# Delta-rule attention and expert layer: key groups 1 and 2 projected in the merging, query group 5 in the recurrence

## The reference, cut to what matters

```python
def _short_conv(x, w):
    K = w.shape[-1]
    L = x.shape[1]
    xp = jnp.pad(x, ((0, 0), (K - 1, 0), (0, 0)))
    y = sum((xp[:, t:t + L, :] * w[:, t] for t in range(K)))
    return jax.nn.silu(y)
...
q = _short_conv(hidden_states @ Wq.T, qconv_w).reshape(B, L, H, -1)
k = _short_conv(hidden_states @ Wk.T, kconv_w).reshape(B, L, H, -1)
v = _short_conv(hidden_states @ Wv.T, vconv_w).reshape(B, L, H, -1)
beta = jax.nn.sigmoid(hidden_states @ Wb.T)
delta, _S = _delta_rule(tr(q), tr(k), tr(v), jnp.swapaxes(beta, 1, 2))
...
short = _fir_conv(v, fir_short_w)
longp = _fir_conv(v, fir_long_w)
paths = (short, longp, delta, v)
gate_in = jnp.concatenate([hidden_states] + [stats(p) for p in paths], -1)
hmid = jax.nn.gelu(gate_in @ gate_w1.T + gate_b1, approximate=False)
logits = hmid @ gate_w2.T + base_bias.reshape(-1)
...
out = sum((probs[..., i, None] * p for i, p in enumerate(paths)))
out = out * jax.lax.rsqrt(jnp.mean(out * out, -1, keepdims=True) + 1e-05) * onorm_w
return out.reshape(B, L, -1) @ Wo.T
```

## Time and profile before

| what | value |
|---|---|
| median of 3 runs | 1901.33 us (1894.56 to 1901.97) |
| the profiled execution's own time | 1894.72 us |
| its span, first to last instruction | 1893.0 us |
| mean granted TensorE clock | 0.904 of full |
| busy: PE, DVE, ACT, POOL | 79%, 69%, 50%, 23% of the span |
| stage B, by the first and last softmax | 428.20 us to 1343.83 us |

### The profile page before, as it was taken

How to read it: one execution, slowest core, us unless ns; L and a number is a source line. 1 busy time by engine, 2 the same in 40 slices (tenths; PEclk the granted TensorE clock), 3 DMA queues, 4 the chain that set the end, 5 groups by cost and what they waited for, 6 DMA issues and landing times. The chain is left out here.

```text
span 1893.0 us, 40332 instructions
## 1 busy us (share of the span) xinstructions
PE 1496.2 (79%) x12507; PEld 1108.8 (59%) x12508; DVE 1315.3 (69%) x3331; ACT 950.1 (50%) x1998; POOL 440.7 (23%) x473
## 2 busy tenths in 40 slices
PE   6775165979999999999999999887436999999800
PEld 3445134747747747657557567476225888888700
DVE  6995155677787887887887887875455555554488
ACT  6772061356555644654655555542443555555434
POOL 6884200000030040040030210300223333333300
PEclk9997585989999999999999999998758999999955
DMA  5558642023243243333333333232524533333295
GB/s 197 190 163 256 154 101 58 3 67 94 71 127 92 62 122 102 78 91 101 87 89 106 95 106 90 79 97 76 196 91 140 192 105 101 104 104 101 77 385 190
DMA packets 297370, 224.34 MB, mean 119 GB/s; under 512 B 173472, under 2 KB 265632, under 8 KB 296960
## 3 DMA queue, kind: packets, MB, share of 16 engines
q1 hardware_dynamic: 225600, 158.84, 29.0%
q0 software_dynamic: 15232, 43.53, 6.4%
q10 hardware_dynamic: 56384, 19.93, 4.1%
HBM read 130.42 MB, written 91.82 MB: 117 GB/s over the span
## 5 line engine op out<-in xcount | busy, mean ns | idle before, releaser
L1462 DVE SCALAR_TENSOR_TENSOR B_conv<-B_ps_x,B_cw,B_conv 128x511 f32<-128x511 f32 (+2 forms) x192 | 143.5, 748 | 65.9 <-ACT B_conv L1176 59.3
L2031 POOL DMA_INDIRECT y_d<-C_yb,C_dest x136 | 132.1, 971 | 232.0 <-ACT C_yb L2142 229.7
L422 POOL DMA_INDIRECT xs_d<-x,slot_u x128 | 133.4, 1042 | 137.4 <-DVE m_acc L1857 100.6
L688 POOL MEMSET B_z<- 128x256 f32 (+4 forms) x40 | 5.5, 191 | 674.6 <-DMA B_z<-scr_a 674.6
L1176 ACT ACTIVATE B_conv<-B_ps_x,B_cw 128x512 f32<-128x512 f32 x64 | 43.7, 683 | 167.6 <-PE B_ps_x L745 167.3
L2261 DVE TENSOR_TENSOR C_av<-C_sg,C_ps_g 128x256 f32<-128x256 f32 x136 | 57.3, 421 | 94.6 <-ACT C_sg L2136 94.6
L2065 PE MATMUL C_ps_g<-C_w_high,C_xt_high 128*128 x272 | 119.5, 439 | 0.4 <-issue 0.4
L745 PE MATMUL B_ps_x<-B_xa,B_wk 128*128 128x512 f32 x128 | 67.5, 655 | 63.8 <-DVE B_sel L1454 44.9
L2273 DVE TENSOR_TENSOR C_avt_low<-C_ps_a,C_avt_high 128x256 fp32r<-128x256 f32 x136 | 57.7, 425 | 83.5 <-ACT C_avt_high L2131 83.5
L2065 PE MATMUL C_ps_g<-C_w_high,C_xt_low 128*128 x272 | 107.7, 396 | 0.0
L2065 PE MATMUL C_ps_g<-C_w_low,C_xt_high 128*128 x272 | 107.0, 393 | 0.0
(11 more groups left out here) (330 smaller groups left out, 4250.6 us busy)
## 6 DMA issues: line engine op xcount, KB each, us to landing
C_xb<-xs_d SPq DMA_DIRECT2D x136, 132.0 KB, 2.1
C_w_high<-y_d SPq DMA_DIRECT2D x12, 1024.0 KB, 14.1
A_band<-fir_long POOLq DMA_DIRECT2D x32, 256.0 KB, 5.9
A_work<-xT SPq DMA_DIRECT2D x16, 512.0 KB, 5.0
v_d<-A_v_tok SPq DMA_DIRECT2D x16, 512.0 KB, 3.5
short_d<-A_sh_tok SPq DMA_DIRECT2D x16, 512.0 KB, 3.2
B_xa<-xT SPq DMA_DIRECT2D x8, 1024.0 KB, 5.8
B_v_tok<-v_d SPq DMA_DIRECT2D x8, 1024.0 KB, 5.5
```

Of the source, the lines that this page charges most:

```text
L422: pool.indirect_dma_start(t["xs_d"][:, :], bass.IndirectOffsetOnAxis(ap=slot_u[:, c:c + 1], axis=0), x1[:, b, j, :], None).then_inc(done, 16)
L1462: V.scalar_tensor_tensor(conv[:, g % 2, k:], X[g % 2][:, :SEQ - k], cw[:, g // 4, gg % CH, 3 - k:4 - k], conv[:, g % 2, k:], ALU.mult, ALU ...
L2031: pool.indirect_dma_start(t["y_d"][:, :], bass.IndirectOffsetOnAxis(ap=dest[:, q:q + 1], axis=0), yb[:, u], None).then_inc(y_out[u], 16)
```

## The change

Every group is taken one place earlier. Groups 1 and 2 of the next pair are projected in `merges`, where two `spin` fillers stood (one of the two came later in it and is moved up), and `group_a(i+2, 1)` on ACT comes with them. In the recurrence, groups 3, 4 and 5 are projected in place of 2, 3 and 4; on DVE the taps of group 1 stand first, and those of groups 4 and 5 later. `stage1b` loses group 5 on all three engines. The `bn` rows of the values are spread over the first block. Three other things are changed:

- The gate's first four products (columns 0 and 1 of half 0, `hidden_from_x`) are made in `stage1b` in place of a `spin(B3, 2)` and a `spin(B3, 3)`.
- POOL's mask waits for the first weighed paths of the mixing (`mixd`) and no longer for the solved blocks read back (`mt_in`).
- PE's first projection of a step no longer waits for the solver's store (`x_out`), and the `spin(X[1], 4)` that ended a step stands behind it.

```diff
                 def mask_at(p):
                     pool.wait_ge(at_kept, 8 * (p + 1))
-                    pool.wait_ge(mt_in[1], 32 * (p + 1))
+                    need(pool, mixd, 4 * (p - 1) + 1)
...
+                def hidden_from_x(i, c):
+                    pe.wait_ge(xg_in[0], 16 * (i + 1))
+                    for k in range(CH):
+                        mm(X[c % 2][:], w1x[:, k, c * P:(c + 1) * P], xg[0][:, k, :], start=k == 0, stop=False)
...
                     turn_norms(p, 0)
-                    project(p, 5)
...
-                            spin(B3, 2)
+                            if g != 6:
+                                spin(B3, 2)
+                        if g == 6 and not first:
+                            pe.wait_ge(taps, 24 * p + 21)
+                            hidden_from_x(p - 1, 0)
...
                         rank(last)
-                        spin(B3, 3)
+                    if not first:
+                        pe.wait_ge(taps, 24 * (p + 1))
+                        hidden_from_x(p - 1, 1)
...
-                    if has_prev:
-                        spin(X[1], 2)
+                    if has_next:
+                        project(i + 1, 1)
...
-                    if has_prev:
-                        spin(X[1], 3)
+                    if has_next:
+                        project(i + 1, 2)
...
-                    if has_next:
-                        project(i + 1, 1)
...
                         if has_next:
-                            project(i + 1, s + 1)
+                            project(i + 1, s + 2)
...
-                        for k in range(CH):
-                            mm(X[c % 2][:], w1x[:, k, c * P:(c + 1) * P], xg[b][:, k, :], start=k == 0, stop=False)
+                        if b or c > 1 or not has_next:
+                            for k in range(CH):
+                                mm(X[c % 2][:], w1x[:, k, c * P:(c + 1) * P], xg[b][:, k, :], start=k == 0, stop=False)
...
                     if has_next:
-                        hold(pe, x_out, 16 * (i + 1))
                         project(i + 1, 0)
+                    if has_prev:
+                        spin(X[1], 4)
                     merges(i, has_prev, has_next)
...
                         at_rest(i + 1)
-                        spin(X[1], 4)
...
                         for k in (1, 2):
                             merge(i + 1, k)
+                    if has_after:
+                        group_a(i + 2, 1)
                     rms(i, 0)
...
-                    for q in range(TPB):
-                        bn(q, 2)
+                    if has_next:
+                        taps_of(i + 1, 1)
+                    bn(0, 2)
                     state(0)
-                    if has_next:
-                        taps_of(i + 1, 1)
+                    bn(1, 2)
                     output(0)
...
                     output(2)
+                    if has_next:
+                        taps_of(i + 1, 4)
...
-                        taps_of(i + 1, 4)
+                        taps_of(i + 1, 5)
```

More of the change, by code:

```diff
@@ L809, in at_products, with stage1b @@
                                 i.then_inc(at_mm, 1)
-                def stage1b(p, last=None):
+                def hidden_from_x(i, c):
+                    pe.wait_ge(xg_in[0], 16 * (i + 1))
+                    for k in range(CH):
+                        mm(X[c % 2][:], w1x[:, k, c * P:(c + 1) * P], xg[0][:, k, :], start=k == 0, stop=False)
+                def stage1b(p, last=None, first=False):
                     if last is not None:
@@ L1008, in gate @@
                     for c in range(HID_CH):
-                        if b == 0 and c == 0:
-                            pe.wait_ge(taps, 24 * (i + 2) if has_next else 24 * (i + 1))
+                        if b == 0 and c == 0 and not has_next:
+                            pe.wait_ge(taps, 24 * (i + 1))
                         if not (b == 0 and c < 2):
                             pe.wait_ge(gelu_ok, 4 * half + c - 1)
-                        for k in range(CH):
-                            mm(X[c % 2][:], w1x[:, k, c * P:(c + 1) * P], xg[b][:, k, :], start=k == 0, stop=False)
+                        if b or c > 1 or not has_next:
+                            for k in range(CH):
+                                mm(X[c % 2][:], w1x[:, k, c * P:(c + 1) * P], xg[b][:, k, :], start=k == 0, stop=False)
                         if c == 0:
@@ L1107, in _ @@
                 turn_betas(0)
-                for g in range(1, 5):
+                for g in range(1, 6):
                     project(0, g)
@@ L1111, in _ @@
                         select(0, g - 2)
-                select(0, 3)
-                stage1b(0)
+                stage1b(0, first=True)
                 at_first(0)
@@ L1213, in stage1b @@
                 def stage1b(p, last=None):
-                    group_a(p, 5)
                     for j in range(4):
@@ L1296, in recur @@
                         group_b(i + 1, 0)
-                        group_a(i + 1, 1)
+                        group_a(i + 1, 2)
                     for s in range(1, TPB):
@@ L1300, in recur @@
                             group_b(i + 1, s)
-                            group_a(i + 1, s + 1)
+                            group_a(i + 1, s + 2)
                         if has_prev and s == 3:
@@ L1396, in _ @@
                     group_b(0, g)
+                group_a(0, 5)
                 root_squares(0, 0)
@@ L1401, in _ @@
                 load_solved(0)
-                for k in range(5):
+                for k in range(3):
+                    merge(0, k)
+                group_a(1, 1)
+                for k in range(3, 5):
                     merge(0, k)
@@ L1492, in stage1b @@
                     keep_k(p, 3)
-                    taps_of(p, 5)
                     dve.wait_ge(beta_ok, 2 * (p + 1))
@@ L1604, in output @@
                                         ALU.mult).then_inc(r_out, 1)
-                    for q in range(TPB):
-                        bn(q, 2)
-                    state(0)
                     if has_next:
                         taps_of(i + 1, 1)
+                    bn(0, 2)
+                    state(0)
+                    bn(1, 2)
                     output(0)
@@ L1618, in recur @@
                         bn(0, 3)
+                    bn(2, 2)
+                    bn(3, 2)
                     residual(1)
@@ L1857, in place @@
                     V.tensor_tensor(m_acc[:], m_acc[:], m_sum[:], ALU.add).then_inc(rt, 1)
-                for g in range(5):
+                for g in range(6):
                     taps_of(0, g)
```

## The result

The changed kernel takes 1908.19 us, median of 9 runs (1905.17 to 1912.86); the kernel before, beside it, 1901.33 (9 runs, 1890.82 to 1903.05). The ratio is 1.0059, with a 95% interval of 1.0039 to 1.0078: slower, where a gain of 1.3% had been forecast. The profiled execution took 1908.19 us, its span is 1906.4 us, the mean granted clock 0.887 (0.904 before).

What follows compares the result with a forecast made beforehand. DVE's own program was taken to bound stage B. Gains of 2.7 + 0.9 + 0.2 = 3.8 us a step, 19 us over five middle steps, plus 5 elsewhere, took 24 us off 1901.33: 1877 us, range 1864 to 1896.

Steps and rivals of the forecast that it cites:

- First taps: Start of a step: projection ahead of the filler lets ACT start sooner; DVE's 1.46 us wait shrinks, gain 0.85 us.
- Merging: Second merge: of 3.4 us gained earlier, 1.5 in hand plus 1.2 from PE starting sooner get through, 2.7 us.
- gains stopped by PE: Rival, chance 0.22: solved blocks no sooner, PE's jump shows, clock takes the recurrence's part; 11.5 us gained, 1890 us.
- Mask: `add_two` (L1725) no longer stands still for POOL's mask, taps not slowed: gain 1.2 us in a middle step.
- Softmax: Gate work about 1.8 us sooner: logits' wait goes, exponentials' wait falls to 0.38 us; gain 1.3 us a step.
- Recurrence and stage 1b: Taps of group 1 wait no more, group 5's move in: 0.9 us gained in the recurrence, 0.2 in `stage1b`.
- The 3 us before `keep_even`: Sign in `stage1b`: without group 5's taps, `keep_even` waits about 3.2 us in place of 1.10.
- The clock: PE ahead of the first solved rows: nearly 4 us wait, clock falls in most steps; by the skill about 1880 us.
- The slow rival: Rival, chance 0.10: clock low from L919 until after the second residual, 36 us lost against 24 gained, 1913 us.
- The sum: Whole kernel: 3.8 us a step, 19 us for five middle steps, 5 us at the ends; 24 us in all.

Runs made afterwards that it cites:

- e1: The changed kernel with the filler put back from behind the first projection to the end of the step: 1881.37 us, ratio 0.9912 to the kernel before.
- e2: The kernel before with only the filler moved behind the first projection, which no longer waits for the memory's outputs: 1914.48 us, ratio 1.0082.
- e11: The changed kernel with the filler in both places, at the end of the step and behind the projection: 1910.12 us, ratio 1.0069.
- e10: The changed kernel with this filler in neither place, not at the step's end nor behind the projection: 1902.08 us, ratio 1.0029.
- e3: The kernel before with only the mask's wait changed, so it starts once the first paths are weighed: 1894.19 us, ratio 0.9991.
- e4: The kernel before with only the gate's four early products, in place of fillers in the stage ahead: 1891.51 us, ratio 0.9966.
- e12: The changed kernel with end filler back but three products instead of four, plus fillers in the gate and ahead of the first solved rows: 1871.85 us, ratio 0.9871.
- e6: The changed kernel with the filler back at the step's end, plus one filler product in each of the gate's two PE waits: 1883.31 us, ratio 0.9920.

## Why the prediction was wrong

- **The step that failed** is *First taps*, "the product comes ahead of the filler", with the 1.2 us in *Merging* for "what PE starts sooner". I asked what ACT gains and not what then stands on PE's path. That path to L891 now holds the jump's idle (2.59 to 3.05 us), the projection, partly at the low clock (2.47 to 3.77 us), and the filler (3.60 to 4.92), which ahead of the jump had cost next to nothing. PE reaches L891 12.1 to 13.9 us into the middle steps, where it had reached L881 at 8.7 to 9.0. The merging was to let 2.7 us of gain through, the 0.85 of the first taps among it; instead the brackets of first taps and merging grew by 3.95 us a step (2.65 to 6.60). e1 and e2 show that the filler's move does it, e11 that the filler on the path is enough, and e10 that the bare jump and its low clock are nearly enough too.
- **The rival "gains stopped by PE"** named the jump on PE, and the second merge's 1.5 us as what was in hand; both are in the trace. I priced it as gains that end (1890), not as a delay larger than them. After the change PE starts L907 at 18.9 to 20.7 us of the middle steps (L897 before: 15.4 to 16.1), where I had allowed it to be no later.
- **Mask**: right in its mechanism (1.23 us in every middle step, the taps as before, 2.32 us for three), wrong for the seventh step, where one instruction still takes 3.40. Alone it shows no gain, on top of e1 0.6%. The 1.2 us were rightly tied to PE's lead in the merging; in e3 it gave out at L919.
- **Softmax**: seen in three of five middle steps (0.38 us left). In the fourth and sixth the waits of 0.62 to 0.65 and 1.13 stay, since the later products ran at the low clock (four took 2.94 us in the gate ahead of the fourth, 1.98 ahead of the third). I had written that all later gate work comes sooner, with no look at what the removed work did for the clock.
- **Recurrence and stage 1b**: 1.1 us forecast, about 0.2 measured (from DVE's restart behind the jump to the wait for the next logits, four steps: 95.1 us before, 94.9 after). The second residual comes 17.6 us after the solved rows in three middle steps and 18.5 in two (754.07 - 735.54 in the step shown), where 16 to 18 was forecast. The 3 us before `keep_even` came as 3.5 to 4.3. The step at 1133.17 that the prediction calls the seventh is the sixth by the softmaxes.
- **The clock**: the fall ahead of the first solved rows came in every middle step, as forecast (L944 takes 3.67 us in all five, behind 3.05 us of idle). The Trainium skill ("TensorE: Matmul & The Clock Gate", "HAM oscillation — how this bites in real kernels") warns of long idle gaps on PE; at this place the trace agrees (3.05 us). The slow rival's amount came as well: it wanted some 10 us more of low clock a step, and by the windows above there are about 11. They lie in other places than it had named, by shorter windows some 4 us behind the jump, 3 in the recurrence, and 3 to 4 in stage 1b and the gate, and the time was not set by their sum (e1 against e11). The forecast had looked for low clock neither behind the jump nor in the gate.
- **The sum**: without the filler's move the same change gives 0.88% (e1; interval 0.55 to 1.21), some 17 us of the 24 forecast. The parts taken alone give less: 0.09% (mask), 0.34% (gate), 0.12% (shift), only the gate's clear of noise.

Left open: where e4's 0.34% lie, and why the low clock behind the jump ends with the projection in some steps of e10 and lasts 10 us in another.

## What to carry to other kernels

Whether a filler is free depends on the place: here, ahead of the loop's jump, it ran in time that the engine would have lost anyway; behind the next projection it delayed the whole chain. When work is taken from a stage of short waits, look at what it did for the clock, and compare the next products' duration before counting the time as won. An edit that frees one wait, such as the mask's, may pay only when the next engine in the chain is early as well, so try parts together and apart. Two faults can also hide each other: take each out alone and both together.

## What the runs showed of the hardware

- At the loop's jump PE idles 2.59 to 3.54 us where no filler is queued ahead of it (the changed kernel, e2, e10), DVE 1.73 to 2.30 us; 2.84 us of queued products hide all but 0.21 us of PE's (e12).
- Idle of 0.76 and 1.26 us, with 0.74 us of products between, was followed by the lower clock ahead of all five middle softmaxes of e4, but of only two of five of the changed kernel. With one filler product in each wait the products behind ran at full speed in every middle step (e6, 1.98 us).
- The lower clock nearly doubles dense products (1.88 to 3.59 us for four of 512 columns), and a filler that is meant to hold the clock up stretches with them (3.70 to 5.33 us).
